# Gate and up's first tokens and first weight pieces prepared inside the output projection

## The reference, cut to what matters

```python
# layer 1: gated attention with a context
x = x + tanh(g_xattn[0]) * attention(layernorm(x), ctx)     # its last step: out @ wo, 2048 -> 512
# layer 2: feed-forward, 2:4 sparse
h = silu(n @ w_gate) * (n @ w_up)                           # n = layernorm(x); 512 -> 2048, twice
h = keep_the_two_largest_of_each_four(h)
x = x + tanh(g_ffn[0]) * (h @ w_down)                       # 2048 -> 512
# layers 3 and 4 (cross attention, quantised feed-forward) stay as they are
```

## Time and profile before

| | us |
|---|---|
| median of 3 runs | 2215.08 (2214.99 to 2220.88) |
| the profiled execution, its own time | 2212.68 |
| its span, first to last instruction | 2210.9 |
| PE busy | 1969.8 (89%) |
| DVE busy | 1369.9 (62%) |
| ACT busy | 1074.2 (49%) |
| POOL busy | 426.6 (19%) |

### The profile page before, as it was taken

One profiled execution on the slowest core, in us unless ns is written; L12 is line 12 of the kernel. 1 busy time (PEld: TensorE's weight loads), 2 busy tenths in 40 slices (PEclk: granted clock), 3 DMA queues, 4 the chain that ended last, 5 costly groups with the idle time before them and its releaser, 6 DMA issues. The chain is left out here.

```text
span 2210.9 us, 33071 instructions
## 1 busy us (share of the span) xinstructions
PE 1969.8 (89%) x10514; PEld 1493.7 (68%) x10514; DVE 1369.9 (62%) x2405; ACT 1074.2 (49%) x2590; POOL 426.6 (19%) x512
## 2 busy tenths in 40 slices
PE   6999479999999999997998999999979988886898
PEld 5888357777666767765786777787768865554454
DVE  6777366766666676764321765645555436885786
ACT  3333156665655666663111622112324417995998
POOL 1111034444434444440000000000000001222111
PEclk9999789999999999998999999999989999998999
DMA  5665762233223241105442412113257623331121
GB/s 216 247 247 218 264 177 81 75 88 89 74 78 87 77 103 41 30 20 191 165 149 72 148 58 69 51 51 95 85 192 260 210 84 104 99 112 49 49 58 43
DMA packets 194087, 254.58 MB, mean 115 GB/s; under 512 B 11782, under 2 KB 144022, under 8 KB 183580
## 3 DMA queue, kind: packets, MB, share of 16 engines
q1 hardware_dynamic: 193948, 252.87, 35.1%
HBM read 152.14 MB, written 100.68 MB: 114 GB/s over the span
## 5 line engine op out<-in xcount | busy, mean ns | idle before, releaser
L937 ACT ACTIVATE at_prob<-at_S,at_bias,at_rq 128x384 f32<-128x384 f32 (+1 forms) x256 | 184.3, 731 | 166.0 <-DVE at_bias L1023 159.8
L1034 DVE TENSOR_TENSOR at_pt_lo<-at_PT,at_pt_hi 128x512 fp32r<-128x512 f32 x224 | 148.9, 689 | 92.5 <-ACT at_pt_hi L944 92.3
L805 POOL TENSOR_SCALAR at_prob<-at_prob,at_rsum 128x384 f32<-128x384 f32 (+1 forms) x256 | 161.2, 643 | 176.4 <-DVE at_rsum L1029 176.3
L864 PE MATMUL at_PT<-c_ident,at_prob 128*128 128x128 f32 x896 | 127.7, 277 | 44.1 <-DVE at_pt_lo L1034 44.1
L1604 ACT ACTIVATE gu_silu<-gu_G 128x512 f32<-128x512 f32 x64 | 38.1, 597 | 244.1 <-PE gu_G L103 234.7
L944 ACT ACTIVATE at_pt_hi<-at_PT 128x512 fp32r<-128x512 f32 x224 | 127.9, 603 | 54.2 <-PE at_PT L864 54.2
L1014 DVE TENSOR_REDUCE at_nmax<-at_S 128x1 f32<-128x384 f32 (+1 forms) x256 | 147.9, 616 | 7.0 <-PE at_S L857 6.6
L864 PEld LDWEIGHTS at_PT<-c_ident,at_prob 128*128 128x128 f32 x896 | 98.0, 140 | 75.0 <-DVE at_pt_lo L1034 70.5
L1642 DVE TENSOR_TENSOR gu_h<-gu_silu,gu_U 128x512 f32<-128x512 f32 x64 | 43.9, 686 | 143.9 <-PE gu_U L103 96.9
L853 PE MATMUL at_S<-at_k_hi,at_q_hi 128*128 128x384 f32 (+1 forms) x256 | 114.0, 445 | 16.9 <-DVE at_q_lo L1039 13.5
L796 POOL TENSOR_TENSOR at_rq<-at_qv,c_minus_half 128x4 f32<-128x4 f32 x64 | 65.2, 1019 | 287.2 <-DVE at_qv L1009 287.2
(11 more groups left out here) (308 smaller groups left out, 5485.3 us busy)
## 6 DMA issues: line engine op xcount, KB each, us to landing
wide<-at_ot SPq DMA_DIRECT2D x64, 256.0 KB, 2.8
wide<-gu_h SPq DMA_DIRECT2D x64, 256.0 KB, 3.2
o_a<-wide SPq DMA_DIRECT2D x14, 1024.0 KB, 4.8
d_a<-wide SPq DMA_DIRECT2D x13, 1024.0 KB, 8.6
keys_hi<-kv_kt_hi SPq DMA_DIRECT2D x8, 1024.0 KB, 4.0
keys_lo<-kv_kt_lo SPq DMA_DIRECT2D x8, 1024.0 KB, 6.0
values_hi<-kv_v_hi SPq DMA_DIRECT2D x8, 1024.0 KB, 8.0
values_lo<-kv_v_lo SPq DMA_DIRECT2D x8, 1024.0 KB, 9.6
```

What stands on the lines that cost most here:

```text
L805: pool.tensor_scalar(prob[u % 2][:, h, 0:n], prob[u % 2][:, h, 0:n], rsum[:, s:s + 1], 1.0, ALU.mult, ALU.mult).then_inc(normed.sem, 1)
L864: last = pe.transpose(bank_of("p", u, kb)[:, h * P:(h + 1) * P], prob[u % 2][:, h, kb * P:(kb + 1) * P], c.ident[:])
L937: act.activation(prob[u % 2][:, h, 0:n], S[h][:, 0:n], ACT.Exp, bias=bias[:, s:s + 1], scale=rq[u % 4][:, h:h + 1], accum_out=sums[:, s:s ...
L1034: dve.tensor_tensor(pt_lo[f % 4][:], bank_of("p", u, kb)[:], pt_hi[f % 4][:].bitcast(F32), ALU.subtract).then_inc(pt_done.sem, 1)
```

## The change

- In the output projection, SP loads gate 0 and up 0 behind the loads of tiles 4 and 5. DVE takes the statistics of tiles 0 to 3 behind `a_lo` of tiles 2 to 5 and normalises them behind `a_lo` of tiles 3 to 6, into a new tile `n_tok`; POOL makes the four powers. PE turns the four tiles behind the product of tile 7. ACT and DVE split the turned tokens at tile 8, the gate piece at tile 9 and the up piece at tile 10.
- The results lie in SBUF rooms that outlive the stage (`tokens_...`: `n_hi`, `n_lo`, `piece_hi`, `piece_lo`).
- To make room, `wo`'s four raw pieces share three rooms: the fourth goes into the first one's room and waits until DVE has split the first. The third room is `n_tok`.
- In gate and up, the first load of `x`, the first layer norm, the 24 awakening matmuls, the 16 transposes, and the splits of tokens and of pieces 0 and 1 are gone; semaphores are set instead. SP's first DMA is piece 2; pieces 2, 3 and 4 and the second pair's `x` are issued without a wait.
- The rooms of pieces are dealt out anew. In the last turn the quarters go in the order 3, 1, 2, 0, so that the rooms for the down projection's weights come free at the same steps as before.

```diff
@@ down @@
+        else:
+            c.make_tokens(nc)
...
+            n_tok = mem.sb("n_tok", [P, TT, D])
             weights = WeightSplit(mem, [(w[i], whole, w_hi[:, 4 * i:4 * i + 4, :],
-                                         w_lo[:, 4 * i:4 * i + 4, :]) for i in range(WP)], raw=WP)
+                                         w_lo[:, 4 * i:4 * i + 4, :]) for i in range(WP)],
+                                  raw=[mem.sb(f"raw{i}", [P, 4, 512]) for i in range(2)] + [n_tok])
...
+            NORM_AT, TURN_AT, PIECE_AT = 3, 7, 9
...
                 load_a(g)
+                if not made and g in (4, 5):
+                    sp.wait_ge(weights.ready, WP)
+                    sp.dma_start(weights.raw[g - 4][:], PIECES[g - 4]).then_inc(piece_arrived[g - 4], 16)
...
                 last.then_inc(Y_full, 1)
+                if not made and g == TURN_AT:
+                    pe.wait_ge(n_normed, TT)
+                    for k in range(DC):
+                        bank_transposes(pe, T[k], n_tok, k, c.ident).then_inc(n_turned, 1)
...
                 act.activation(a_hi[g % 2][:], a[g % 2][:], ACT.Copy).then_inc(hi_done, 1)
+                if not made and g == TURN_AT + 1:
+                    for k in range(DC):
+                        act.wait_ge(n_turned, k + 1)
+                        act.activation(c.n_hi[:, k, :], T[k][:], ACT.Copy).then_inc(n_hi_done, 1)
+                if not made and g in (PIECE_AT, PIECE_AT + 1):
+                    i = g - PIECE_AT
+                    act.wait_ge(piece_arrived[i], 16)
+                    act.wait_ge(weights.ready, WP)
+                    act.activation(c.piece(c.piece_hi, i), every_fourth(weights.raw[i]), ACT.Copy).then_inc(piece_hi_done, 1)
...
+                if not made:
+                    if 0 <= g - NORM_AT < TT:
+                        first_normalise(g - NORM_AT)
+                    if 0 <= g - 2 < TT:
+                        first_statistics(g - 2)
+                    first_pieces(g)
@@ gate_up @@
-                [tile_room("hi", n), mem.sb(f"{n}_hi3", [P, DC, 4, P], F32R)[:]] for n in "gu"}
+        w_hi = {n: [c.piece(c.piece_hi, "gu".index(n)), weight_room(down_w_hi, n, 1), tile_room("hi", n),
+                    weight_room(down_w_hi, n, 0)] for n in "gu"}
...
+        def quarter(q, more):
+            return q if more else (3, 1, 2, 0)[q]
...
-            sp.dma_start(x[:], scr.x[0][0]).then_inc(x_arrived.sem, 16)
-            for n in range(WP):
-                if n == 2:
-                    sp.wait_ge(*T_full.at(0, DC))
-                if n >= 3:
+            sp.sem_inc(x_arrived.sem, 16)
+            for n in range(AHEAD, WP):
+                if n >= 5:
                     sp.wait_ge(w_ready, n if n >= 6 else n - 2)
...
-            pe.wait_ge(*x_arrived.at(0, 16))
-            keep_awake(pe, G[0], c, AWAKE)
-            turn_xn(0)
+            pe.sem_inc(T_full.sem, DC)
             turns(pe, body)
...
-            split_hi_weights(act, 0)
-            split_n(0)
-            split_hi_weights(act, 1)
+            act.sem_inc(hi_done.sem, DC)
+            act.sem_inc(w_hi_ready, AHEAD)
...
-            ln.vector(dve, 0, T_full.at(0, 0))
-            split_lo_weights(dve, 0)
-            split_n(0)
-            split_lo_weights(dve, 1)
+            dve.sem_inc(ln.stats.sem, ln.steps)
+            dve.sem_inc(ln.xn_ready.sem, TT)
+            dve.sem_inc(lo_done.sem, DC)
+            dve.sem_inc(w_ready, AHEAD)
```

More of the change, by code:

```diff
@@ L1103, in down @@
             Y = [mem.bank(f"Y{i}") for i in range(2)]
+            T = [mem.bank(f"T{k}") for k in range(DC)]
+            n_bn = mem.sb("n_bn", [P, TT, 6])
+            n_mv = mem.sb("n_mv", [P, TT, 2])
+            n_ve = mem.sb("n_ve", [P, TT])
+            n_rstd = mem.sb("n_rstd", [P, TT])
+            n_bn_done = mem.sem("n_bn_done")
+            n_ve_done = mem.sem("n_ve_done")
+            n_rstd_done = mem.sem("n_rstd_done")
+            n_normed = mem.sem("n_normed")
+            n_turned = mem.sem("n_turned")
+            n_hi_done = mem.sem("n_hi_done")
+            n_lo_done = mem.sem("n_lo_done")
+            piece_arrived = [mem.sem(f"piece_arrived{i}") for i in range(2)]
+            piece_hi_done = mem.sem("piece_hi_done")
+            piece_lo_done = mem.sem("piece_lo_done")
+            PIECES = [io[f"L0_ffn_w_{name}"].rearrange("(k p) n -> p k n", p=P)[:, :, 0:512] for name in ("gate", "up")]
+            NORM_AT, TURN_AT, PIECE_AT = 3, 7, 9
         first_arrived = [mem.sem(f"first_arrived{r}{j}") for r in range(1 if made else 2) for j in range(WP)]
@@ L1240, in _ @@
                     pool.tensor_tensor(rstd[:, r], ve[:, r], c.minus_half[:, 0:1], ALU.pow).then_inc(rstd_done, 1)
+        if not made:
+            @block.gpsimd
+            def _(pool):
+                for t in range(TT):
+                    pool.wait_ge(n_ve_done, t + 1)
+                    pool.tensor_tensor(n_rstd[:, t:t + 1], n_ve[:, t:t + 1], c.minus_half[:, 0:1],
+                                       ALU.pow).then_inc(n_rstd_done, 1)
         @block.tensor
@@ L1406, in gate_up @@
     with ExitStack() as ctx:
+        ctx.enter_context(c.tokens)
         c.make_down(nc)
@@ L1529, in body @@
                     for t in range(TT):
-                        sp.dma_start(scr.wide[turn, t, :, 4 * q:4 * q + 4, :],
+                        own = 4 * quarter(q, more)
+                        sp.dma_start(scr.wide[turn, t, :, own:own + 4, :],
                                      h[q % 2][:, :, t * P:(t + 1) * P]).then_inc(h_stored[q % 2].sem, 16)
@@ L1539, in _ @@
             ln.rstd_ready.start(pool)
-            with pool.Fori(0, PAIRS) as turn:
+            pool.sem_inc(ln.rstd_ready.sem, 1)
+            with pool.Fori(1, PAIRS) as turn:
                 ln.gpsimd(pool, turn, c.minus_half)
@@ L1565, in body @@
                                 pe.wait_ge(*lo_done.at(turn, k + 1))
-                            last = three_passes(pe, bank[:], [(w_hi[n][q][:, k, j, :], w_lo[n][q][:, k, j, :],
+                            own = quarter(q, more)
+                            last = three_passes(pe, bank[:], [(w_hi[n][own][:, k, j, :], w_lo[n][own][:, k, j, :],
                                                                n_hi[:, k, :], n_lo[:, k, :])],
@@ L2502, in __init__, with make_tokens, far, piece @@
         self.ones = mem.sb("ones", [P, P])
+    def make_tokens(self, nc):
+        self.tokens = ExitStack()
+        def far(name, shape, dt=F32):
+            return self.tokens.enter_context(nc.sbuf_tensor("tokens_" + name, shape, dt, side="right"))
+        self.n_hi = far("n_hi", [P, DC, TOK], F32R)
+        self.n_lo = far("n_lo", [P, DC, TOK], F32R)
+        self.piece_hi = [far(f"piece_hi{i}", [P, DC, 512], F32R) for i in range(2)]
+        self.piece_lo = [far(f"piece_lo{i}", [P, DC, 512], F32R) for i in range(2)]
+    def piece(self, rooms, i):
+        return rooms[i][:].rearrange("p k (j q) -> p k j q", j=4)
     def make_down(self, nc):
```

32 lines of the change are left out of this document (27 added, 5 removed).

## The result

| | before | after |
|---|---|---|
| median, first comparison | 2217.98 us (2214.99 to 2222.79, 4 runs) | 2196.28 us (2193.82 to 2198.36, 4 runs) |
| median, second comparison | 2214.64 us (2210.10 to 2220.54, 22 runs) | 2198.87 us (2196.83 to 2200.13, 6 runs) |
| the profiled execution, and its span | 2212.68, 2210.9 us | 2196.85, 2195.1 us |

The ratio is 0.990 in the first comparison (95% interval 0.9875 to 0.9924) and 0.9922 in the second (0.9908 to 0.9936). The kernel became faster by 16 to 22 us. The time forecast was 2200.4 us.

The account below looks back on a forecast made before the run. PE, busy 89% of the span, was taken as the bound. -15.5 + 2.2 + 0 - 1.4 = -14.7 us took 2212.7 to 2198.0, or 2200.4 from the 2215.1 median; range 2197.5 to 2203, slower rivals to 2205.5.

Parts of the forecast that it names:

- The sum: Parts 1 to 6 added against the profiled execution: -14.7 us, from 2212.7 to 2198.0 us.
- Part 1: Start of gate and up: first product 0.5 us behind SP's first DMA, 15.5 us earlier.
- (a): PE's branches at the start of gate and up: first product at most 4.3 us behind, +3.8 us, 2204.2; chance 0.13.
- Part 2: Output projection behind tile 7: the 16 moved transposes cost PE 2.2 us, ACT's and DVE's new work 0.
- Part 3: Output projection: wo's fourth weight piece is delayed by at most 4.1 us; cost 0, bound 0.6 us.
- Part 4: First products of gate and up: PE at half clock for 3.4 us, a loss of 1.6 us, range 0 to 2.4.
- Part 5: First turn: the chain from piece 5's split to step 8 starts at 29.4 instead of 30.8 us, 1.4 us gained.
- Part 6: Later turns of gate and up: turns 2 and 3 as before, the last turn's new order of quarters costs 0.
- (b): Start of gate and up: four transfers at once make pieces 3 and 4 late, chain 5 us later, 2205.4; chance 0.08.
- (c): Start of gate and up: PE's clock doesn't fall or returns at once, -1.6 us, 2198.8; chance 0.07.
- (d): Gate and up: without awakening matmuls the clock stays low; to step 10 it is +50 - 15, 2250; chance 0.02.
- (e): Projection tiles 7 to 10: PE waits for ACT's or DVE's new work; 8 us lost gives 2208.4; 0.04 with unnamed costs.

Follow-up runs that it names:

- e_signals: The changed kernel with DVE's two signals that PE waits for set first in its list instead of last of nine: 2200.79 us, ratio 0.9943.
- the pairs with 16 and 20 products: Dummy matmuls ending the output projection: 16 or 20 on the changed kernel (2199.01, 2201.07 us), and with piece 7's split at step 8 and signals first (2192.27, 2191.89 us).
- e_after: The changed kernel once more without an edit, beside the kernel before: 2198.87 us, ratio 0.9922.
- e_turn2: The changed kernel with the 16 transposes behind tile 7 of the output projection made twice: 2205.16 us, ratio 0.9949.
- e_late8: The changed kernel with piece 7 split at step 8 of the first turn instead of step 7: 2195.37 us, ratio 0.9903.
- e_two: The changed kernel with piece 7 split at step 8 and DVE's two signals first, no dummy products: 2193.85 us, ratio 0.9909.

## Why the prediction was right, and where it was wrong

**The sum.** Forecast were -14.7 us from projection to step 8; measured -14.6 and -14.2. By parts, with the two profiles:

- Part 1, start: the wait behind SP's first DMA was taken as 0.5 us and is 1.15. That is inside what rival (a) priced, and the gain at the seam is 14.8 us instead of 15.5. Of the 0.65 us too few, 0.3 are the order of DVE's signals (`e_signals`); what the rest is isn't shown.
- Part 2, transposes: 2.2 forecast, 1.9 measured, and 1.8 for 16 more. No wait of PE at tiles 8 to 11; PE's only wait among the products of the projection is 1.7 us at tile 2, as before.
- Part 3, fourth piece of `wo`: it was issued at 1027.85, behind the first split, and its own split ended at 1041.6, 13.4 us after the first product instead of 12.8. PE wants it at 16.3. It cost nothing.
- Part 4, clock: low for 3.2 and 3.8 us, where 3.4 were taken. Its cost of 1.6 us is 1.8 by the pairs with 16 and 20 products. That 3.4 was right and 5.2 wrong is partly luck: the prediction chose between its two rows by the length of the hole, and in other kernels with a hole of the same length (5.5 to 5.8 us) the clock stayed low for 3.3 to 6.1 us.
- Part 5, chain: the splits of pieces 2 to 5 were forecast for 13.1, 18.5, 24.0 and 29.4 us after the first product, and ended at 12.8, 18.3, 23.7 and 29.1 in the first profile. From there to step 8 it took 33.6 us, as before. With the clock in it, the first turn became 1.7 and 1.3 us shorter; forecast were 1.4.
- Part 6 is not shown to be anything but 0: step 8 to the first product of the down projection took 319.8 and 320.5 us against 321.0.

**The rivals.** (a) didn't come: the first product was 1.15 us behind SP's DMA, not 4.3, and its releaser is DVE's signal. The rule of the Trainium skill (Runtime: NRT & Kernel Launch, Instruction fetch mechanics), a stall at a branch to a page that isn't loaded, would have put PE's start later than that signal; no run here shows such a stall, and with the signals moved PE started 0.85 us after SP. (b) didn't bite: ACT split pieces 3 and 4 right behind the silu of their steps, without a wait for their loads. (c) and (d) fell: the clock fell and came back. (e) fell too: PE had no new wait in the projection. The margin at tile 9, put at 1.2 us, was 0.87.

**The step that failed** is the last one, from the sum to a median and its range. The profiled execution was forecast at 2198.0 us and took 2196.85. To this the forecast added 2.4 us, since before's profiled execution ran so far below its median; in the changed kernel it was the other way round, with medians 0.6 us (2196.28 to 2196.85) and 1.0 us (2198.87 to 2199.83) below the profiled executions. So of the 4.1 us between the forecast of 2200.4 and the first median of 2196.28, this step makes 3.0 and the sum before it 1.15. One execution's place among its like doesn't carry over to another kernel's. And the range allowed "some 1 us between measurements". The kernel before alone ran from 2210.1 to 2220.5 us in 22 runs. Its median was 2218.0, 2214.6, 2216.1 and 2213.2 in four comparisons (the 2215.1 that the forecast starts from is of three of the first one's four runs), and the changed kernel's was 2196.3 and 2198.9 in two. By these medians one comparison is uncertain by 2 to 3 us, not 1. With that term the low end would have been near 2195, and both medians inside. The profile of after shows such differences too: its span lies 15.8 us under that of before, of which 14.6 come from the change's place. The projection's first product came 2.1 us earlier (1028.2 against 1030.3): 1.7 of it lie before SP's first DMA of that stage, and 0.4 in the stage's start. From step 8 to the down projection's first product and from there to the cross stage it was 1.2 and 0.8 us shorter, and the last two stages were 2.9 us longer (386.0 against 383.1, from the first score product to the last product). Of all this only the stage's start and the order of the last turn are code that the change touches, and `e_after` shows no gain there (12.6 us for that start, against 12.3 before).

**What stays open.** The medians are 21.7 us apart in the first comparison and 15.8 in the second; the second has more runs and agrees with the trace (14.2 to 14.6 us at its place), and nothing but the spread of the runs was found for the first. The spread itself has a sign: in the 22 runs of the kernel before, the six with a mean granted clock of 0.964 took 2210.1 to 2213.6 us, and the six with 0.961 or less took 2216.3 to 2220.5. Which of the two causes the other isn't shown, and the clock of before's runs in the first comparison isn't known. Open is too why the median with the transposes doubled is 6 us above the changed kernel's, when their place in the projection costs 1.8.

## What to carry to other kernels

When two strings of preparation end together at an engine's first work, ask what remains if each is taken away alone: here each half bought 1.5 or 4.7 us up to step 8 and the whole 14.2 to 14.6, so a half would have been thrown away as useless. After an engine starts earlier, the next bound is a chain of its own, and moving one split out of the chain's way (piece 7 behind the store) bought another 5.5 to 5.9 us there, of which 3.5 showed in the median. And the range of a forecast needs a term for the spread of the runs themselves, taken from more than three of them.

## What the runs showed of the hardware

**The length of a hole doesn't alone decide over PE's clock.** With holes of 1.99 and 2.35 us (16 products) it fell to half just behind the first product; with 2.02 and 2.32 us (20 products) it stayed full. These are two profiles of each kind, so that chance isn't excluded. Nor does the fall come at a fixed distance behind PE's last work, or the return at a fixed distance behind its first:

| | fall, us after the end of PE's last work | low behind the first product, us | first turn, us |
|---|---|---|---|
| after, first profile | 2.2 | 3.2 | 62.7 |
| `e_after` | 2.8 | 3.8 | 63.1 |
| `e_signals` | 2.7 | 4.0 | 63.0 |
| `e_turn2` | 4.7 | 5.7 | 63.8 |
| `e_late8` (piece 7 moved) | 2.3 | 3.3 | 57.2 |
| `e_two` (piece 7 moved) | 4.8 | 6.1 | 58.6 |

In all six the hole was 5.5 to 5.8 us long. The times of the fall and of the return are worked out from the granted clock in windows of 1 us. In the two kernels where the clock fell late it also came back late, and there the first turn was 1.1 and 1.4 us longer than the shortest of its kind. Before the change it had fallen 4.4 us after the last product. What sets the time of the fall isn't shown.

**The cross stage takes a different time in each execution, along with its granted clock.** No kernel here changes it. Its first 195 us, PE alone, in before, then in the changed kernel, then in the one with 20 dummy products:

```profile
1823.40:2018.40 195.00, 170.64 (x1540) 0.98 0.30 98
```

```profile
1804.70:1999.70 195.00, 170.64 (x1514) 0.96 0.29 96
```

```profile
1809.30:2004.30 195.00, 173.53 (x1451) 0.91 0.29 95
```
